# A seven-stage image pipeline: point-wise product on split operands, box sums on one engine

## The reference, cut to what matters

```
x = x + L0(gn(x))   # w_eff = sum_k sparsemax(pooled @ gate_w.T + gate_b)[k] * expert_w[k];  1x1 conv with w_eff
x = x + L1(gn(x))   # below
x = x + L2(gn(x))   # attention over channels: q2, k2 squared and normalised, value and output products
x = x + L3(gn(x))   # 3x3 box mean

# L1
h = depthwise_3x3(x, dw_w) + dw_b
h = relu(bn(h, bn1));  h = where(max|h| over the image < 4.0, 0, h)      # per channel
h = pointwise_1x1(h, pw_w) + pw_b
h = relu(bn(h, bn2));  h = where(max|h| over the image < 0.001, 0, h)    # per channel
```

## Time and profile before

| | us |
|---|---|
| median of 3 runs (lowest, highest) | 1684.85 (1683.39, 1685.81) |
| profiled execution, its own time | 1683.19 |
| span of the profiled execution | 1681.4 |
| busy: PE / DVE / ACT / POOL | 1543.4 / 1452.5 / 1369.0 / 421.4 |
| one steady step, from `gn_avg` to `gn_avg` | 49.1 |

### The profile page before, as it was taken

How to read it: one execution, slowest core, us unless ns; L and a number is a source line. 1 busy time by engine, 2 the same in 40 slices (tenths; PEclk the granted TensorE clock), 3 DMA queues, 4 the chain that set the end, 5 groups by cost and what they waited for, 6 DMA issues and landing times. The chain is left out here.

```text
span 1681.4 us, 26750 instructions
## 1 busy us (share of the span) xinstructions
PE 1543.4 (92%) x8190; PEld 1144.9 (68%) x8190; DVE 1452.5 (86%) x2530; ACT 1369.0 (81%) x3496; POOL 421.4 (25%) x269
## 2 busy tenths in 40 slices
PE   3569999999999999999999999999999999998994
PEld 2247777677777767777776777777677777766773
DVE  5867799999989999998999999899999989998646
ACT  3368988888888888888888888888888888878872
POOL 1111212233321223332122333212233321223224
PEclk8689999999999999999999999999999999999997
DMA  4000011100111110011111001111100111000000
GB/s 143 20 20 20 20 39 39 39 20 20 39 38 38 38 38 19 19 38 38 38 38 38 19 19 38 38 38 38 38 19 19 38 38 39 20 20 20 20 20 39
DMA packets 21058, 55.58 MB, mean 33 GB/s; under 512 B 2321, under 2 KB 3345, under 8 KB 21010
## 3 DMA queue, kind: packets, MB, share of 16 engines
q1 hardware_dynamic: 20914, 54.98, 9.3%
q10 hardware_dynamic: 96, 0.00, 0.0%
HBM read 29.29 MB, written 25.69 MB: 33 GB/s over the span
## 5 line engine op out<-in xcount | busy, mean ns | idle before, releaser
L769 DVE SCALAR_TENSOR_TENSOR h<-xpad,dw_sb,h 128x784 f32<-128x784 f32 x512 | 534.3, 1097 | 1.1
L540 PE MATMUL tile_ps<-wqk,xn_parts 128*112 128x512 f32 x1344 | 363.6, 425 | 0.0
L540 PEld LDWEIGHTS tile_ps<-wqk,xn_parts 128*112 128x112 f32 x1344 | 234.6, 175 | 80.2
L1223 POOL TENSOR_SCALAR xpad<-x,gn_r,gn_s 128x784 f32<-128x784 f32 x64 | 64.8, 1020 | 784.1 <-DVE gn_s L700 784.1
L448 PE MATMUL conv_ps<-h,pw_masked 128*128 128x392 f32 x512 | 183.5, 502 | 42.6 <-DVE x L805 37.1
L582 PE MATMUL tile_ps<-k,xT 112*128 112x256 f32 x896 | 205.1, 388 | 7.7 <-ACT xT L1029 7.7
L582 PEld LDWEIGHTS tile_ps<-k,xT 112*128 112x128 f32 x896 | 174.2, 195 | 40.1 <-issue 8.4
L963 ACT ACTIVATE junk<-x 128x784 bf16<-128x784 f32 x192 | 163.1, 851 | 40.6 <-DVE x L805 20.7
L570 PE MATMUL conv_ps<-x,mixed 128*128 128x392 f32 (+1 forms) x512 | 177.4, 499 | 2.2 <-ACT mixed L997 1.1
L448 PEld LDWEIGHTS conv_ps<-h,pw_masked 128*128 128x128 f32 x512 | 93.4, 192 | 111.6 <-DVE x L805 38.7
L448 PE MATMUL conv_ps<-xn_parts,w_out 128*128 128x392 f32 x768 | 153.1, 348 | 0.0
(11 more groups left out here) (143 smaller groups left out, 3020.5 us busy)
## 6 DMA issues: line engine op xcount, KB each, us to landing
x<-x SPq DMA_DIRECT2D x32, 784.0 KB, 4.3
out<-x SPq DMA_DIRECT2D x32, 784.0 KB, 3.5
expert_sb<-expert_rows SPq DMA_DIRECT2D x8, 256.0 KB, 5.5
x<-w_qk SPq DMA_DIRECT2D x1, 512.0 KB
x<-w_vT SPq DMA_DIRECT2D x1, 256.0 KB
x<-w_ln SPq DMA_DIRECT2D x1, 256.0 KB
pw_sb<-pw_wT SPq DMA_DIRECT2D x1, 256.0 KB
gmean<-group_mean SPq DMA_DIRECT2D x1, 64.0 KB, 4.0
```

The source lines that it names most:

```text
L540: mm = nc.tensor.matmul(bank, xn2_parts[:, u, i, m * TOK:(m + 1) * TOK], wqk[:, v, i, :], start=False, stop=(i == J - 1 and u == 1))
L769: ins = nc.vector.scalar_tensor_tensor(acc, view, scalar, acc, ALU.mult, ALU.add)
```

## The change

- The point-wise product is computed by parts: `pw_parts` (high and low part of the weights, made in the setup) and `h_parts` (high and low part of the masked h). For each half POOL makes the high part, mask times h (`h_high`), and VectorE the low part (`h_low`). `pw_masked` and its two POOL instructions are gone.
- The mask is made per half, in two instructions.
- All box sums are on VectorE, each instruction over both halves (1568 pixels); `make_x4` waits for the whole.
- On VectorE `make_x3` comes ahead of the taps and the box sums.
- The taps alternate strictly between the halves.
- `sparsemax` has 12 instructions where it had 14.
- Buffers: `over` is one buffer for both sums, `junk` is shorter, and ScalarE has a few waits on its own earlier work.

```diff
@@ TensorE
             def pointwise(C_, halves):
-                pe.wait_ge(h_ready.sem, h_ready.at(C_))
-                pe.wait_ge(pw_masked_ready.sem, pw_masked_ready.at(C_))
+                pe.wait_ge(h_lo.sem, h_lo.at(C_))
                 for j in halves:
                     wait_free((C_ - 2, x3_ready, j + 1), (C_ + 1, x1_ready, j + 1))
-                    conv_tile(j, [(pw_masked[:, i, :], h[:, C_.odd, i, :]) for i in range(J)]).then_inc(pw_mm.sem, 1)
+                    conv_tile(j, by_parts(pw_parts, h_parts)).then_inc(pw_mm.sem, 1)
@@ VectorE
-        TAP_TURNS = [(0, 0)] + [turn for n in range(1, TAPS) for turn in ((0, n), (1, n - 1))] + [(1, TAPS - 1)]
+        TAP_TURNS = [(j, n) for n in range(TAPS) for j in range(J)]
+                parts_of(pw_parts, pw_raw)
...
-            def h_mask(C_):
-                dve.wait_ge(h_over_sum.sem, h_over_sum.at(C_))
+            def h_mask(C_, j):
+                dve.wait_ge(h_over_sum.sem, h_over_sum.at(C_, j + 1))
...
+                nc.vector.scalar_tensor_tensor(hmask[:, j:j + 1], h_over[:, j:j + 1], ones[:, 0:1], zeros[:], ALU.mult,
+                                               ALU.is_gt).then_inc(hmask_step.sem, 1)
+            def h_low(C_, j):
+                dve.wait_ge(h_hi.sem, h_hi.at(C_, j + 1))
...
+                nc.vector.scalar_tensor_tensor(h_parts[:, 1, j, :], h[:, C_.odd, j, :], hmask[:, j:j + 1],
+                                               h_parts[:, 0, j, :].bitcast(F32), ALU.mult,
+                                               ALU.subtract).then_inc(h_lo.sem, 1)
@@ GpSimd
-            def box_sums(F):
-                pool.wait_ge(x3pad_ready.sem, x3pad_ready.at(F))
-                for n in range(BOX_STEPS):
...
-            def mask_weights(C_):
+            def h_high(C_, j):
                 if (C_ - 1).active:
                     pool.wait_ge(pw_mm.sem, pw_mm.at(C_ - 1))
+                pool.wait_ge(hmask_step.sem, hmask_step.at(C_, j + 1))
                 hold(pool, "pool")
+                nc.gpsimd.tensor_scalar(h_parts[:, 0, j, :], h[:, C_.odd, j, :], hmask[:, j:j + 1], 0.0, ALU.mult,
+                                        ALU.add).then_inc(h_hi.sem, 1)
```

More of the change, by code:

```diff
@@ L29 @@
 PACKED = EXPERTS // STRIPS
-GATE_STEPS = 17
+GATE_STEPS = 15
 XW = HW + 2
@@ L131, in build @@
         bn1_sb, bn2_sb = params[:, 4:8, :], params[:, 8:12, :]
-        pw_sb = sb("pw_sb", [P, J, C])
+        pw_parts = sb("pw_parts", [P, 2, J, C], F32R)
         wqk = sb("wqk", [P, 2, J, 2 * C], F32R)
@@ L290, in build @@
         x3pad_ready = sig("x3pad_ready", J)
-        box_step = [sig(f"box_step{j}", BOX_STEPS) for j in range(J)]
+        box_step = sig("box_step", BOX_STEPS)
         x4_ready = sig("x4_ready", J)
@@ L914, in step @@
                 if B.active:
-                    depthwise(B, slice(5, 9))
+                    depthwise(B, slice(1, 3))
+                if C_.active:
+                    h_mask(C_, 0)
+                    h_mask(C_, 1)
+                if F.active:
+                    box_sums(F, range(2))
+                if C_.active:
+                    h_low(C_, 0)
+                if F.active:
+                    box_sums(F, range(2, BOX_STEPS))
+                if C_.active:
+                    h_low(C_, 1)
                 if B.active:
-                    depthwise(B, slice(9, 10))
+                    depthwise(B, slice(3, 10))
                 if D.active:
@@ L1072, in sum_over_h @@
                     act.wait_ge(hmask_step.sem, hmask_step.at(B - 1))
-                    act.wait_ge(h_over_sum.sem, h_over_sum.at(B - 1, j + 1))
+                    act.wait_ge(y_over_sum.sem, y_over_sum.at(B - 1))
+                if j:
+                    act.wait_ge(h_over_sum.sem, h_over_sum.at(B, j))
                 act.wait_ge(h_ready.sem, h_ready.at(B, j + 1))
-                nc.scalar.activation(over[:, 0, j, :], h[:, B.odd, j, :], ACT.Relu, bias=below[:, 0:1],
+                nc.scalar.activation(over[:], h[:, B.odd, j, :], ACT.Relu, bias=below[:, 0:1],
                                      accum_out=h_over[:, j:j + 1]).then_inc(h_over_sum.sem, 1)
@@ L1081, in sum_over_y @@
                     act.wait_ge(ymask_step.sem, ymask_step.at(C_ - 1))
-                    act.wait_ge(y_over_sum.sem, y_over_sum.at(C_ - 1, j + 1))
+                act.wait_ge(h_over_sum.sem, h_over_sum.at(C_))
+                if j:
+                    act.wait_ge(y_over_sum.sem, y_over_sum.at(C_, j))
                 act.wait_ge(y_ready.sem, y_ready.at(C_, j + 1))
-                nc.scalar.activation(over[:, 1, j, :], x2[:, C_.odd, j, :], ACT.Relu, bias=below[:, 1:2],
+                nc.scalar.activation(over[:], x2[:, C_.odd, j, :], ACT.Relu, bias=below[:, 1:2],
                                      accum_out=y_over[:, j:j + 1]).then_inc(y_over_sum.sem, 1)
@@ L1250, in step @@
                     normalise_x1(A, B, C_)
-                if F.active:
-                    box_sums(F)
                 if C_.active:
-                    mask_weights(C_)
+                    for j in range(J):
+                        h_high(C_, j)
             run(pool, step)
```

100 lines of the change are left out of this document (46 added, 54 removed).

## The result

The changed kernel takes 1731.97 us (median of 4 runs, 1730.23 to 1733.51) against 1685.07 (1683.39 to 1685.81) for the kernel before: 1.0279 times as long, 95% interval 1.0262 to 1.0297. It is slower by 47 us where 23 were forecast. The time lies inside the range given (1668 to 1735), near its upper end, and the sign is right; the size is not.

The account below looks back on a forecast made before the run. The prediction took a DVE-ACT-DVE chain of 49.1 us between `gn_avg`s as the bound. Its terms summed to +0.8 us a step, +23 us over 29 steps, giving 1708 us, with a range of 1668 to 1735.

Parts of the forecast that it names:

- The ring: Closed chain from one `gn_avg` to the next, DVE to `qk_eps`, then ACT, then DVE: 49.1 us, said to set the step.
- The terms: The change's parts costed on a steady step from `gn_avg` to `gn_avg`, summing to +0.8 us a step, +23 us over 29.
- Rival 5: The parts of the steady step cancel, an error of 0.8 us leaving no change: 1685 us; chance 0.09.
- the two small gains: On DVE in a steady step: the shorter `sparsemax`, -0.33 us, and the strictly alternating tap order, -0.12 us.
- the mask's wait: DVE, ahead of the box sums, waits 0.4 us for half 1's sum; with 0.1 for the second mask, +0.5.
- `h_high`'s hold-up: POOL's two `h_high` instructions delay DVE's second mask and box sums: +1.35 us a step, bounds 0 and 3.0.
- The product by parts: Point-wise product on PE: 1.1 us a step saved, then lost waiting that much longer for `xT`, so 0.
- rival 4: TensorE's clock falls after about 2.2 us idle ahead of the last transposes: 1.3 us a step, 1746 us; chance 0.05.
- it is wrong if `gn_avg` waits for PE: Sign to check in the profile after: `gn_avg` on DVE waiting for PE would show the prediction wrong.
- Rival 1: POOL's `h_high` falls into waits and doesn't hamper DVE: -0.55 us a step, 1669 us, faster; chance 0.10.
- Rival 2: PE sets the pace, so the point-wise saving and the `x3` wait come off: -2.4 a step, 1615 us; chance 0.05.
- rival 3: `h_high` on POOL is as slow as POOL's box sums: +2.4 us a step, 1755 us; chance 0.05.

Follow-up runs that it names:

- the filler kernel: The changed kernel plus 16 small bf16 matmuls on PE between the point-wise product and the last transposes, into unread PSUM columns: 1699.75 us.
- the kernels with steps of 46.7: Kernel before with all box sums on VectorE (1614.52 us); that with `reciprocal_sums` two taps earlier (1614.48); everything but the split product, same move (1615.18).

## Why the prediction was right, and where it failed

**The ring: right.** `reciprocal_sums` two taps earlier gave 86 us in the changed kernel and 22 in the one before, so DVE's stretch from `gn_avg` to `qk_eps` was the bound, and costing the change on it was the right frame.

**The terms: right, and their sum nearly so.** With the clock kept (the filler kernel) the step is 49.68 us against 49.12: +0.56 where +0.8 was forecast, and 1699.75 is 17 us above before where +23 was forecast. (Rival 5 puts the terms at 5.9 and 7.1; those with a minus sign add up to 6.25, and the sum of +0.8 has it right.) In order along the ring:
- `gn_avg` to `xn_parts`: 10.91 us against 11.11 before, -0.20 (forecast -0.33 for `sparsemax`).
- From there to `qk_eps`: 22.60 against 21.61, +0.99 (forecast +1.25 without the two small gains). In it the mask's wait is 0.26 to 0.27 in a steady step (forecast 0.4); box sums take 1.78 to 1.79 (forecast 1.8); `h_high`'s hold-up is 0.87 - 0.21 = 0.66 at the second mask and 2.39 - 1.78 = 0.61 at the second box sum, 1.27 together (forecast 1.35). The first box sum wasn't lengthened, as I had expected it to be; the delay sat in the mask ahead of it.
- `qk_eps` to `gn_avg`: 16.17 against 16.40, -0.23 (forecast -0.12 for the order of taps).
`h_high` took 0.92 us without contention, so float32r output costs POOL nothing next to `xpad`'s 0.99. `qk_eps` stood 33.5 us behind `gn_avg` there, and 33.9 in the changed kernel; 33.6 was forecast. The last step but one took 23.06 us against 20.14, +2.9, for which +3 was forecast.

**"The product by parts: ... PE saves 1.1 us a step, and then waits that much longer for `xT` ...: 0" is the step that failed**, with its "at an unchanged clock". The saving is 26.9/32 = 0.84 us a step, and the wait came out as described, 2.1 us ahead of the last transposes. I had seen that this wait collects PE's idle time in one place, and wrote it down as rival 4, but gave it 0.05 because the clock had stayed full through gaps of 1.3 us. That is a good deal shorter than 2.2, and the only longer wait shown ended in a fall. Between bounds of 1.3 (no fall) and 3.47 (a fall) a wait of 2.2 is undecided, and 0.05 was no fair share for it. The size of the effect was about right: 1.3 us a step was priced, and a step with a fall takes 51.12 in place of 49.65, +1.5, in some 22 steps: 32 us, which is 1731.97 - 1699.75.

**How the fall reaches the end.** `mixed_conv` is 1.70 us longer, PE reaches `small_ps` late, `gn_avg` waits 0.99, and the next `xn_parts` comes 11.29 us behind `gn_avg` in place of 10.91. So PE joins the ring in those steps. The prediction's check "it is wrong if `gn_avg` waits for PE" pointed at the right place. Where PE has spare time behind the fall, as with `h_high` doubled, nothing reaches the end.

**The rivals.** Rival 1 (no hold-up by `h_high`) is out by 1.27 us measured in the step and +35 us on doubling. Rival 2 (PE the bound) is out for these two kernels by the moves of `reciprocal_sums`, while it is true of the kernels with steps of 46.7; rival 3 by `h_high`'s 0.92 us; rival 5 by the interval. The outcome is the forecast's ring with rival 4 on top of it: +15 to +17 (1699.75 against 1685.07, or against the 1683 measured beside it) and +32. The two were treated as one or the other, while nothing kept both from being true.

**What the change is made of.** Box sums on VectorE alone: -68 us. Everything but the product: -58. The split product: +106.5, of which 32 are the clock; the other 74 are 2.65 us in each step (49.65 - 47.0), about the 1.9 of the two `h_low` and the 1.27 of hold-up less 0.3 that `pw_masked` had cost there. It saves PE 0.84 us a step, which PE can't use at steps of 49.1 and more. These figures hold in this order of taking the change apart; with the box sums' move as the last step it is -18, and all that goes ahead of it +66. The prediction had both signs in its sum but didn't single out the half that is a gain.

**What stays open.** Why about the same wait lets the clock fall in most steps of one kernel and in few of another. Within a kernel its place in time decides (`h_high` doubled). The changed kernel fits that: its steps take 51.12 us and its falls are 51.2 apart, so they move by only 0.1 us a step against the wait, begin up to 1.4 us behind its end and then stop for two steps. But with `reciprocal_sums` two taps later only falls that begin within about 0.1 us of the end of the wait occur, and what PE does around the wait differs there too. No run changed that alone, so the forecast for another kernel has to carry both outcomes.

## What to carry to other kernels

Find the ring that sets the step, and cost every edit on it: here PE was 92% busy, and giving it less to do, at the price of more work on VectorE, made the kernel slower. Look for idle time that an edit collects in one place on TensorE; where it exceeds the longest gap that the trace shows at full clock, price the fall in the forecast itself, not as a side case, and take off what TensorE has to spare behind it. And take a change apart before judging it: one half of this one is worth 4%, and the other half costs more than that.

## What the runs showed of the hardware that I had not expected

- An idle time of 1.8 to 2.3 us on TensorE, once in about 51 us, let the granted clock fall to its lower level for 3.4 us in some steps and not in others, at equal waits (1.84, 2.13 and 2.29 us in three kernels). At 1.3 us (the filler) and 1.6 us (`mixed_conv` split) it never fell in the steady part.
- A fall costs nothing where TensorE has a wait of 1.6 us behind it: with `h_high` doubled, steps take 50.8 to 50.9 us with a fall or without.
- VectorE's instruction with one operand in PSUM (`x3`, 1.03 us) runs beside GpSimd's box sums without loss, while the tap behind it takes 2.65 in place of 0.95.
- Being held up by a GpSimd instruction of 0.92 us costs VectorE 0.6, not 0.92.
- GpSimd writing float32r (784 columns, 0.92 us) is no slower than `xpad`, which writes float32 (0.99).
